# Expert rows packed block by block: fixed addresses for token loads and result stores in a routed transformer

## The chip, the cores and the metric

The kernel runs on one core of one Trainium2 chip. The metric is the device time of one execution in microseconds (us). The kernel before took 2116.01, 2119.6 and 2120.47 us in three runs, median 2119.6. Float32 is the type of inputs and outputs, a part of the attention works in bfloat16.

## The reference

The input is a batch of 4 sequences of 1024 tokens with 128 features. Two layers follow each other, each with a modulated layer norm before both halves. Layer 0 has attention with 16 heads over a window of 64 tokens, and then a mixture of 8 experts; layer 1 has full attention, then a block of its own with attention over the batch, and a mixture of 8 experts again. The part at hand is the mixture:

```python
logits = xf @ Wg.T + bg
probs = softmax(logits)
tp, ti = top_k(probs, 2)
h = gelu(einsum('td,efd->tef', xf, W1) + b1)      # DF = 512 in layer 0, 256 in layer 1
y = einsum('tef,edf->ted', h, W2) + b2
out = einsum('ted,te->td', y, w)                  # w: the two chosen probabilities
```

Every token needs only its two experts, so a kernel may send each token to those two and leave the other six out.

## The kernel before, in words

The engines are PE (matrix multiply), DVE (vector), ACT (scalar), POOL (GpSimd) and SP (which only issues transfers). The program is a row of stages with a barrier between them: start, `window_attention_stage` (78 to 619 us of the profile), the expert stages moe0b (620 to 746) and moe0c (752 to 881), `gather_qkv_stage`, full attention, cross attention, `last_norm_stage` (1797 to 1871), moe1b (1872 to 1962), moe1c (1967 to 2064) and the last gather (2068 to 2112).

**Parts and rows.** The batches are split in two parts of HB = 2 batches. A normalised token row is scattered twice, once per chosen expert, to the DRAM array `moe_rows` by an indirect DMA of POOL that takes a column of slots (`self.slot`) as row numbers: 16 scatters of 128 tokens per batch (`scatter`, `scatter_one`, lines 1531 to 1550). In `moe_rows` every expert of a part has a region of SPAN = 2048 rows of its own. So a batch's slot is known as soon as that batch is counted: `place` (line 1474) adds the expert's base, the count of the batches and tiles before, and the rank, and casts to integers. Its semaphore `placed` releases the batch's scatters. Unused rows must hold finite numbers, so `clear_rows` fills the array with zeros in the window attention, 19 DMAs of 960 KB on POOL's queue.

**Blocks.** `tabulate` (line 1505) runs once per part, after its second batch. It makes from the counts a table of NBK = 23 blocks of BR = 256 rows: which expert, and at which row the block begins. `block_stage` (line 1567) works through them: SP loads for each block the token rows (line 1604) and the expert's weights (line 1608, 578 KB in layer 0), PE turns the tokens (L1621), multiplies (L1632, L1642), ACT applies gelu (L1678), DVE copies (L1693, L1703, L1705), and ACT stores the result over the token rows (L1664), three blocks behind. Buffers for six blocks (XB, WBUF) let SP run ahead. Expert and row are read into registers by `load_four` (line 1560), four blocks at a time: one TENSOR_LOAD and eight register operations. SP calls it twice per four blocks, for experts and for rows, ACT once, for the rows of its stores.

**Work beside blocks.** Each expert stage takes an object whose methods run beside the blocks, called with the block's number j. In moe0b that is `RouteBeside` (line 1094): it routes the last batch (the norm, logits, probabilities, `compare`, `order`, `weights`, `place`, `tabulate`, spread over j = 0 to 13), and POOL scatters the last two batches, 11 scatters ahead of the second norm's `deviation`, 5 behind it, and 16 when the last batch is placed. In moe0c and moe1c it is `GatherBeside` (32 gathers of the first part's results), in moe1b `ScatterBeside` (line 1203, 32 scatters of the second part). POOL's method starts with the stage.

**The other scatters.** In the window attention DVE's and POOL's loops run over g, the groups of heads; `routed_at(g)` gives batch b - 1 a window of 32 steps. Batch 0's 16 scatters are issued in the window of b = 1, batch 1's in that of b = 2 (the last, 482 to 619 us), one per step between two multiplications of `probs` (L1061). In last_norm POOL scatters batches 0 and 1 as soon as each is placed, while DVE goes on with batches 2 and 3.

**Order.** Every engine executes its own list in the order of the code; nothing is reordered by a planner. Within `RouteBeside` the number j says beside which block a routing step stands.

## Time and profile before

| what | us |
|---|---|
| median of three runs (2116.01, 2119.6, 2120.47) | 2119.6 |
| the profiled execution | 2118.16 |
| its span | 2116.3 |
| PE busy | 1646.2 (78%) |
| DVE busy | 1357.7 (64%) |
| ACT busy | 1157.6 (55%) |
| POOL busy | 547.7 (26%) |

The sum of the prediction is made against the profiled execution, whose span can be read in the trace. Busy shares are averages over stages with different limits; the granted clock of PE was 0.874 of full speed in the mean. POOL's busy time has the issue of its indirect DMAs in it, SP's issues are not counted as busy. The software queue, which carries POOL's DMAs, moved 36.52 MB in 12464 packets, 5.0% of the 16 DMA engines' span.

### The profile page before, as it was taken

What the parts mean: (1) busy time and instruction counts of PE and PEld (TensorE: products, weight loads), DVE (VectorE), ACT (ScalarE), POOL (GpSimd) and SP (SyncE); (2) the same over time, 40 slices, a digit from 0 to 9 for tenths busy, and PEclk for the clock granted to TensorE, in tenths of its full rate; (3) what the DMA queues carried; (4) which work ended last, traced back from release to release, by engine and by line L of the source; (5) the groups of instructions that cost most, each with busy time, mean ns of one, the idle gap of its engine ahead of it and who ended that gap; (6) DMA issues with size and microseconds to landing.
All of it is one profiled execution on the core that took longest, in us unless ns stands there. A gap on an engine that the chain in (4) does not pass through costs nothing. (4 is left out here: it accounts for less than half of the span.)

```text
span 2116.3 us, 35460 instructions
## 1 busy us (share of the span) xinstructions
PE 1646.2 (78%) x11792; PEld 972.3 (46%) x11792; DVE 1357.7 (64%) x3360; ACT 1157.6 (55%) x3025; POOL 547.7 (26%) x620
## 2 busy tenths in 40 slices
PE   7799999999978849736999999999999543527280
PEld 3487778777768738611222222222222333416270
DVE  5654656666553305457999999999996468714062
ACT  3466766666644314331888888888888440202030
POOL 2133423525323244341001001001000100561505
PEclk8899999999989969865999999999999865558695
DMA  5144211111126446331000000000000000026362
GB/s 166 54 161 154 104 30 36 43 29 49 32 81 201 142 150 205 94 111 63 21 26 17 26 22 21 25 18 25 25 10 2 1 4 0 29 84 188 105 192 62
DMA packets 91569, 148.64 MB, mean 70 GB/s; under 512 B 18772, under 2 KB 59476, under 8 KB 91388
## 3 DMA queue, kind: packets, MB, share of 16 engines
q1 hardware_dynamic: 65676, 97.78, 15.8%
q0 software_dynamic: 12464, 36.52, 5.0%
q10 hardware_dynamic: 13248, 12.06, 1.7%
q8 instruction: 96, 1.57, 0.3%
q14 instruction: 85, 0.70, 0.1%
HBM read 82.25 MB, written 47.93 MB: 62 GB/s over the span
## 5 line engine op out<-in xcount | busy, mean ns | idle before, releaser
L2276 DVE TENSOR_REDUCE q_max<-s_ps 128x1 f32<-128x1024 f32 x512 | 598.1, 1219 | 14.0 <-PE s_ps L2167 6.6
L2257 ACT ACTIVATE probs<-s_ps 128x512 f32<-128x512 f32 x1024 | 535.5, 603 | 124.6 <-PE s_ps L2188 124.5
L2167 PE MATMUL s_ps<-k_stack,q_stack 64*128 64x512 bf16 x1024 | 351.4, 397 | 16.5 <-PEq L98 8.1
L2188 PE MATMUL s_ps<-q_stack,k_stack 64*128 64x512 bf16 x1024 | 319.7, 384 | 20.0 <-ACT probs L2257 15.6
L2202 PE MATMUL o_ps<-probs,v_aug 128*32 128x512 f32 x2048 | 273.6, 606 | 0.7 <-ACT probs L2257 0.7
L2188 PEld LDWEIGHTS s_ps<-q_stack,k_stack 64*128 64x128 bf16 x1024 | 78.4, 94 | 334.0 <-ACT probs L2257 282.1
L939 ACT ACTIVATE probs<-s_biased,s_min 128x128 f32<-128x128 f32 (+1 forms) x512 | 197.7, 391 | 39.7 <-DVE s_min L1032 38.3
L1061 POOL TENSOR_TENSOR probs<-probs,p_rsum 128x512 f32<-128x512 f32 x128 | 132.9, 1038 | 326.7 <-DVE p_rsum L1038 325.6
L804 PE MATMUL score_ps<-k_pad,q_bd 128*128 128x128 f32 x1024 | 145.9, 286 | 0.0
L1032 DVE CUSTOM_DVE_ANT_0 s_biased<-score_ps,nbias 128x128 f32<-128x128 f32 (+1 forms) x512 | 115.8, 282 | 40.4 <-PE score_ps L804 37.9
L1792 POOL CAST neg_max_parts<-neg_max 16x128 bf16<-16x128 f32 x32 | 9.0, 281 | 474.9 <-DVE neg_max L2284 474.9
L2167 PEld LDWEIGHTS s_ps<-k_stack,q_stack 64*128 64x128 bf16 x1024 | 77.3, 94 | 113.0 <-DVE q_max L2276 104.4
L804 PEld LDWEIGHTS score_ps<-k_pad,q_bd 128*128 128x128 f32 x1024 | 125.2, 192 | 7.4 <-issue 1.0
L962 DVE TENSOR_SCALAR q_bd<-proj_ps,qscale 64x512 f32<-64x512 f32 x64 | 48.5, 757 | 107.0 <-PE proj_ps L784 103.9
L1044 DVE COPY probsT<-probsT_ps 128x512 f32<-128x512 f32 x128 | 86.6, 677 | 35.9 <-PE probsT_ps L815 35.2
L939 ACT ACTIVATION_READ_ACCUMULATOR probs<-s_biased,s_min 128x1 f32 x512 | 98.0, 191 | 0.0
L889 ACT ACTIVATE q_bd<-proj_ps,qscale 64x512 f32<-64x512 f32 x64 | 43.7, 683 | 84.4 <-PE proj_ps L784 84.4
L1678 ACT ACTIVATE moe0c_hid<-moe0c_hps,moe0c_wblock 128x256 f32<-128x256 f32 x92 | 39.9, 473 | 86.5 <-PE moe0c_hps L1632 42.1
L815 PE MATMUL probsT_ps<-ident,probs 128*128 128x128 f32 x512 | 77.9, 275 | 4.6 <-POOL probs L1061 4.6
L830 PE MATMUL o_ps<-probsT,v_shift 128*64 128x64 f32 x1024 | 73.4, 234 | 9.2 <-ACT oT L947 8.6
L815 PEld LDWEIGHTS probsT_ps<-ident,probs 128*128 128x128 f32 x512 | 62.1, 142 | 37.8 <-issue 31.6
L1548 POOL DMA_INDIRECT moe_rows<-hk,moe_slot x64 | 66.7, 1042 | 43.4 <-DVE moe_slot L1494 28.8
(355 smaller groups left out, 2957.4 us busy)
## 6 DMA issues: line engine op xcount, KB each, us to landing
moe_rows<-zero_rows POOLq DMA_DIRECT2D x19, 960.0 KB
moe0b_wblock<-in_L_ffn_blocks SPq DMA_DIRECT2D x23, 578.0 KB
moe0c_wblock<-in_L_ffn_blocks SPq DMA_DIRECT2D x23, 578.0 KB
v_shift<-v_tiles SPq DMA_DIRECT2D x32, 256.0 KB
v_shift<-v_tiles SPq DMA_DIRECT2D x32, 224.0 KB
qk_parts_dram<-qk_parts SPq DMA_DIRECT2D x16, 384.0 KB
q_stack<-qk_parts_dram SPq DMA_DIRECT2D x192, 32.0 KB
k_stack<-qk_parts_dram SPq DMA_DIRECT2D x192, 32.0 KB
```

Of the source, the lines that this page charges most:

```text
L804: m = nc.tensor.matmul(sp_[g % 2][:, i, :], qbd[:, h % 2, j, :], kk[:, h % 2, BLK * j:BLK * j + P], start=True, stop=True)
L815: m = nc.tensor.transpose(tp[:, i, :], pr[:, k % 3, i, :], K.ident[:])
L830: m = nc.tensor.matmul(op[a * BLK:(a + 1) * BLK, i, :], src[:, a * HD0:(a + 1) * HD0], pt[:, k % 2, i, a * BLK:(a + 1) * BLK], start=True, ...
L939: r = nc.scalar.activation(pr[:, g % 3, i, own], sb_[:, g % 2, i, own], ACT.Exp, scale=-1.0, bias=mn[:, g % 4, i:i + 1], accum_out=sm[:, g ...
L1032: q = v.tensor_tensor_reduce(sb_[:, g % 2, i, own], sp_[g % 2][:, i, own], nbias[:, h % PAIRS, own], 1.0, 3e38, ALU.add, ALU.min, mn[:, g ...
L1044: v.tensor_copy(pt[:, k % 2], tp[:]).then_inc(pt_out, 1)
L1061: nc.gpsimd.tensor_tensor(pb, pb, bc(ri[:, g % 4, :], 2, P), ALU.mult).then_inc(normed, 1)
L2167: mm = nc.tensor.matmul(s1[u % 2][:, c * CH:(c + 1) * CH], qs[head_rows(m), quad % 4, j, qt * P:(qt + 1) * P], ks[head_rows(m), quad % 4, ...
L2188: nc.tensor.matmul(bank_of("exp", 4 * k + pos)[:], ks[head_rows(m), quad % 4, j, kt * P:(kt + 1) * P], qs[head_rows(m), quad % 4, j, half ...
L2202: m = nc.tensor.matmul(op[32 * h:32 * h + 32, :], va[:, quad % 2, kt, h, :], pr[:, k % 2, h, :], start=(kt == 0), stop=(kt == TPB - 1))
L2257: nc.scalar.activation(pr[:, k % 2, HEADS[pos], :], bank_of("exp", n)[:], ACT.Exp).then_inc(sm["exp"], 1)
L2276: v.tensor_reduce(mx[:, h % 4, col:col + 1], s1[u % 2][:], AX.X, ALU.max).then_inc(sm["maxed"], 1)
```

## The change

The rows of a part are packed block by block: expert after expert, each rounded up to whole blocks of 256 rows. Block j of part p then always begins at row (23 p + j) x 256, which is a constant of the program; only the expert, and with it the weights, is still picked by register.

- `moe_rows` has 2 x 23 x 256 = 11776 rows instead of 36480. The fill takes 23 DMAs of 256 KB.
- A slot is final only when both batches of a part are counted, since an expert's first block depends on the experts before it. `place` computes a rank within the expert (`rel`, in floats). `tabulate` computes the first row of each expert, and then per batch the slots (multiply with the choice, reduce, add), with a new semaphore `final` that the scatters wait for. The table keeps the experts alone.
- `load_four` is called once per four blocks by SP, and not at all by ACT. Token loads and stores have fixed addresses.
- In the window attention all 32 scatters of batches 0 and 1 move into the last window, at steps 2 to 31, with two behind the loop.
- `RouteBeside`: the routing steps stand closer: shift_logits at j = 7 (was 8), probabilities and compare at 8 (9), order and weights both at 9 (10 and 11), place and tabulate both at 11 (12 and 13). POOL computes both deviations first, and then issues all 32 scatters.
- In every expert stage POOL waits for the fourth token load (`x_in[3]`) before its work beside.
- In last_norm the code of POOL is unchanged, but its scatters now wait for `final`, so for `tabulate` of part 0.

The diff, without declarations of sizes and constants:

```diff
 NBKP = -(-NBK // 4) * 4
-PROWS = E * SPAN + (E - 1) * BR
-ROWS = 285 * P
-ZR = 5
+PROWS = NBK * BR
+ROWS = 2 * PROWS
+ZR = 4
 STEPS_OF = SPAN // BR
...
 
-        FILLS = ROWS // P // ZR // 3
+        FILLS = ROWS // P // ZR
 
         def clear_rows(pool, n):
 
             rows = K.moe_rows.rearrange("(p r) d -> p (r d)", p=P)
-            part = rows[:, 3 * n * ZR * D:3 * (n + 1) * ZR * D].rearrange("p (k z) -> p k z", k=3)
-            pool.dma_start(part, bc(zero[:], 1, 3)).then_inc(cleared, 16)
+            pool.dma_start(rows[:, n * ZR * D:(n + 1) * ZR * D], zero[:]).then_inc(cleared, 16)
 
...
                             N2.deviation(pool, b)
-                        if b >= 1 and at < 2 * TPB:
-                            if b == 1 and at == 0:
+                        if b == HB and at >= 2:
+                            if at == 2:
                                 pool.wait_ge(cleared, 16 * FILLS)
-                            M.scatter_one(pool, N2, b - 1, at)
+                            M.scatter_one(pool, N2, *divmod(at - 2, 2 * TPB))
+                for n in range(2 * TPB - 2, 2 * TPB):
+                    M.scatter_one(pool, N2, 1, n)
                 M.wait_scattered(pool, HB)
...
             N2.normalised_odd(dve, b)
+        elif j == 7:
+            M.shift_logits(dve, b, self.raw_logits)
         elif j == 8:
-            M.shift_logits(dve, b, self.raw_logits)
-        elif j == 9:
             M.probabilities(dve, b)
             M.compare(dve)
-        elif j == 10:
+        elif j == 9:
             M.order(dve)
+            M.weights(dve, b)
         elif j == 11:
-            M.weights(dve, b)
-        elif j == 12:
             M.place(dve, b, self.prior)
-        elif j == 13:
             M.tabulate(dve, 1)
...
             m.then_inc(M.logit_mm, 1)
-        elif j == 11:
+        elif j == 10:
             pe.wait_ge(M.chose, b + 1)
...
                              bias=M.affine[:, 1:2], scale=M.affine[:, 0:1]).then_inc(self.turn_out, 1)
-        elif j == 9:
+        elif j == 8:
             M.exponentials(act, b)
-        elif j == 12:
+        elif j == 11:
             act.wait_ge(M.prefixed, b + 1)
...
         N1.deviation(pool, b)
-        for n in range(11):
-            M.scatter_one(pool, N2, b - 1, n)
         N2.deviation(pool, b)
-        for n in range(11, 2 * TPB):
-            M.scatter_one(pool, N2, b - 1, n)
-        for n in range(2 * TPB):
-            M.scatter_one(pool, N2, b, n)
+        for k in (b - 1, b):
+            for n in range(2 * TPB):
+                M.scatter_one(pool, N2, k, n)
         M.wait_scattered(pool, B)
...
-        self.hot = K.sb(name + "_hot", [P, 2, TPB, E], ctx=st)
+        self.hot = K.sb(name + "_hot", [P, HB, 2, TPB, E], ctx=st)
-        self.place_f = K.sb(name + "_place", [P, 2, TPB], ctx=st)
+        self.rel = K.sb(name + "_rel", [P, HB, 2, TPB], ctx=st)
+        self.base_f = K.sb(name + "_base", [P, 2, TPB], ctx=st)
-         self.counted, self.placed, self.chain, self.scattered) = K.sems(
+         self.counted, self.placed, self.chain, self.scattered, self.final) = K.sems(
             st, name + "r", "router_in", "ones_set", "logit_mm", "shifted", "exp", "chosen", "prefix_mm", "counted", "placed",
+            "chain", "scattered", "final")
...
         dve.wait_ge(self.prefixed, b + 1)
-        ts = slice(b * TPB, (b + 1) * TPB)
-        part, first = divmod(b, HB)
-        base = self.cum[:, b - 1, :, TPB] if first else self.steps[:, part * E:(part + 1) * E]
-        step(dve, v.tensor_copy(self.tot[:, b % 2, :, 0], base))
+        if b % HB:
+            step(dve, v.tensor_copy(self.tot[:, b % 2, :, 0], self.cum[:, b - 1, :, TPB]))
+        else:
+            step(dve, v.memset(self.tot[:, b % 2, :, 0], 0.0))
         dve.wait_ge(self.counted, b + 1)
...
                                   ALU.add))
-        step(dve, v.tensor_tensor(self.picked[:], bc(self.slots[:], 1, 2), self.hot[:], ALU.mult))
-        step(dve, v.tensor_reduce(self.place_f[:], self.picked[:], AX.X, ALU.add))
-        v.tensor_copy(self.slot[:, :, ts], self.place_f[:]).then_inc(self.placed, 1)
+        step(dve, v.tensor_tensor(self.picked[:], bc(self.slots[:], 1, 2), self.hot[:, b % HB], ALU.mult))
+        v.tensor_reduce(self.rel[:, b % HB], self.picked[:], AX.X, ALU.add).then_inc(self.placed, 1)
 
...
         v, step = self.nc.vector, self.step
-        base, marks = self.steps[:, part * E:(part + 1) * E], self.steps[:, 2 * E:2 * E + STEPS_OF]
-        number = self.steps[:, 2 * E + STEPS_OF:]
+        marks, number = self.steps[:, 0:STEPS_OF], self.steps[:, STEPS_OF:]
         blocks, first, upto = (self.nb[:, i, :] for i in range(3))
-        passed, spent = self.le[:, 0], self.le[:, 1]
-        expert, row, rest = (self.tf[:, i, :] for i in range(3))
-        step(dve, v.tensor_tensor(first, self.cum[:, (part + 1) * HB - 1, :, TPB], base, ALU.subtract))
-        step(dve, v.tensor_tensor(self.over[:], bc(first, 2, STEPS_OF), bc(marks, 1, E), ALU.is_gt))
+        passed, expert = self.le[:], self.tf[:]
+        dve.wait_ge(self.placed, (part + 1) * HB)
+        total = self.cum[:, (part + 1) * HB - 1, :, TPB]
+        step(dve, v.tensor_tensor(self.over[:], bc(total, 2, STEPS_OF), bc(marks, 1, E), ALU.is_gt))
         step(dve, v.tensor_reduce(blocks, self.over[:], AX.X, ALU.add))
         g4 = self.pairs[:].rearrange("p (a b) -> p a b", a=E)
         step(dve, v.tensor_tensor(g4, bc(blocks, 1, E), self.low[:].rearrange("p (a b) -> p a b", a=E), ALU.mult))
         step(dve, v.tensor_reduce(first, g4, AX.X, ALU.add))
-        step(dve, v.tensor_tensor(upto, first, blocks, ALU.add))
+        v.tensor_tensor(upto, first, blocks, ALU.add)
+        step(dve, v.tensor_scalar(first, first, float(BR), float(part * PROWS), ALU.mult, ALU.add))
+        for i in range(HB):
+            b = part * HB + i
+            step(dve, v.tensor_tensor(self.picked[:].rearrange("p c t e -> p (c t) e"), bc(first, 1, 2 * TPB),
+                                      self.hot[:, i].rearrange("p c t e -> p (c t) e"), ALU.mult))
+            step(dve, v.tensor_reduce(self.base_f[:], self.picked[:], AX.X, ALU.add))
+            v.tensor_tensor(self.slot[:, :, b * TPB:(b + 1) * TPB], self.base_f[:], self.rel[:, i], ALU.add
+                            ).then_inc(self.final, 1)
+        dve.wait_ge(self.final, (part + 1) * HB)
         step(dve, v.tensor_tensor(passed, bc(upto, 1, NBK), bc(number, 2, E), ALU.is_le))
-        step(dve, v.tensor_tensor(spent, passed, bc(blocks, 1, NBK), ALU.mult))
-        v.tensor_reduce(expert, passed, AX.X, ALU.add)
-        step(dve, v.tensor_reduce(rest, spent, AX.X, ALU.add))
-        step(dve, v.tensor_tensor(rest, number, rest, ALU.subtract))
-        step(dve, v.tensor_scalar(rest, rest, float(BR), float(part * PROWS), ALU.mult, ALU.add))
-        step(dve, v.scalar_tensor_tensor(out=row, in0=expert, scalar=float(SPAN), in1=rest, op0=ALU.mult,
-                                         op1=ALU.add))
+        step(dve, v.tensor_reduce(expert, passed, AX.X, ALU.add))
         step(dve, v.tensor_scalar(expert, expert, float(E - 1), None, ALU.min))
-        step(dve, v.tensor_copy(self.table[:, part, :, 0:NBK], self.tf[:, 0:2, :]))
+        step(dve, v.tensor_copy(self.table[:, part, 0:NBK], expert))
 
     def scatter(self, pool, N, b, first, last):
 
-        pool.wait_ge(self.placed, b + 1)
+        pool.wait_ge(self.final, b + 1)
         N.wait_normalised(pool, (b + 1) * TPB)
...
         if n == 0:
-            pool.wait_ge(self.placed, b + 1)
+            pool.wait_ge(self.final, b + 1)
             N.wait_normalised(pool, (b + 1) * TPB)
...
             def _(pool):
+                pool.wait_ge(x_in[3], 16)
                 beside.gpsimd(pool)
 
             @block.sync
             def _(sp):
-                experts, rows = {}, {}
+                experts = {}
                 for j in range(NBK):
                     if j % 4 == 0:
-                        experts.update(load_four(nc, mybir.EngineType.SP, M.table[0:1, part, 0], j, E - 1))
-                        rows.update(load_four(nc, mybir.EngineType.SP, M.table[0:1, part, 1], j, ROWS - BR))
+                        experts.update(load_four(nc, mybir.EngineType.SP, M.table[0:1, part], j, E - 1))
                     if j >= XB:
                         sp.wait_ge(turned, j - XB + 1)
-                    sp.dma_start(xi[:, j % XB], K.moe_rows[bass.ds(rows.pop(j), BR), :].rearrange("(p a) d -> p a d", a=H)
+                    sp.dma_start(xi[:, j % XB], K.moe_rows[(part * NBK + j) * BR:(part * NBK + j + 1) * BR, :].rearrange("(p a) d -> p a d", a=H)
                                  ).then_inc(x_in[j % XB], 16)
...
             def _(act):
-                rows = {}
-
                 def store(k):
 
                     act.wait_ge(y_out, k + 1)
-                    act.dma_start(K.moe_rows[bass.ds(rows.pop(k), BR), :].rearrange("(p a) d -> p a d", a=H),
+                    act.dma_start(K.moe_rows[(part * NBK + k) * BR:(part * NBK + k + 1) * BR, :].rearrange("(p a) d -> p a d", a=H),
                                   ys[:, k % YB]).then_inc(stored[k % YB], 16)
 
                 for j in range(NBK):
-                    if j % 4 == 0:
-                        rows.update(load_four(nc, mybir.EngineType.Activation, M.table[0:1, part, 1], j, ROWS - BR))
                     if j >= 3:
```

How this moves instructions, first on POOL's queue in moe0b (`n0ba_rstd` and `n0bb_rstd` are the two deviations, the DMAs are scatters). Before:

```order
L147 TENSOR_TENSOR n0ba_rstd<-n0ba_ve,neghalf 128x8 [waits n0a_var_eps]
L1548 DMA moe_rows<-hk,moe0_slot 36480x128 [waits start_scales,start_cols_out,start_x_in3]
L1548 DMA moe_rows<-hk,moe0_slot 36480x128 x10
L147 TENSOR_TENSOR n0bb_rstd<-n0bb_ve,neghalf 128x8 [waits start_exp]
L1548 DMA moe_rows<-hk,moe0_slot 36480x128 x5
L1548 DMA moe_rows<-hk,moe0_slot 36480x128 [waits start_scales,start_cols_out,start_x_in3]
L1548 DMA moe_rows<-hk,moe0_slot 36480x128 x15
```

After:

```order
L147 TENSOR_TENSOR n0ba_rstd<-n0ba_ve,neghalf 128x8 [waits n0a_var_eps,win_probsT_out]
L147 TENSOR_TENSOR n0bb_rstd<-n0bb_ve,neghalf 128x8 [waits start_exp]
L1546 DMA moe_rows<-hk,moe0_slot 11776x128 [waits start_scales,start_cols_out,moe0r_final]
L1546 DMA moe_rows<-hk,moe0_slot 11776x128 x15
L1546 DMA moe_rows<-hk,moe0_slot 11776x128 [waits start_scales,start_cols_out,moe0r_final]
L1546 DMA moe_rows<-hk,moe0_slot 11776x128 x15
```

(Semaphores are shared between stages, so a wait can bear the name of an earlier stage's.) The groups of 11, 5 and 16 have become one row of 32, all behind `final`, and the second deviation no longer has scatters ahead of it.

Then SP's queue at the start of moe0b, where the ISA rows are register operations. Before:

```order
L1563 TENSOR_LOAD moe_table
L1563 ISA x8
L1563 TENSOR_LOAD moe_table
L1563 ISA x8
L1604 ISA
L1604 DMA moe0b_xin<-moe_rows 128x256
L1608 ISA
L1608 DMA moe0b_wblock<-in_L_ffn_blocks 128x1156
```

After:

```order
L1561 TENSOR_LOAD moe_table
L1561 ISA x8
L1602 DMA moe0b_xin<-moe_rows 128x256
L1606 ISA
L1606 DMA moe0b_wblock<-in_L_ffn_blocks 128x1156
```

One load of the table with its eight operations is gone ahead of the first token load, and one register operation at each token load. The same holds for every fourth block; over the program SP has 24 such loads instead of 48.

## Rows read from the trace of the kernel before

**Rows 1.** The page, first line: the span.
```profile
span 2116.3 us, 35460 instructions
```

**Rows 2.** Timeline of POOL in moe0b: start us, length us, instruction, idle before.
```profile
633.96 1.06 POOL L1548 DMA_INDIRECT moe_rows<-hk,moe_slot  x1 [0.20 <-issue]
...
646.70 0.95 POOL L1548 DMA_INDIRECT moe_rows<-hk,moe_slot  x1 [0.30 <-issue]
...
693.46 0.96 POOL L1548 DMA_INDIRECT moe_rows<-hk,moe_slot  x1 [28.78 <-DVE moe_slot L1494]
...
712.48 0.95 POOL L1548 DMA_INDIRECT moe_rows<-hk,moe_slot  x1 [0.30 <-issue]
```

**Rows 3.** Windows in moe0b: us, busy us (count) per engine, PEclk, DMA share, GB/s.
```profile
634.00:654.00 20.00, 12.73 (x76) 11.82 (x75) 5.30 (x12) 6.44 (x16) 10.60 (x11) 0.84 0.56 187
...
658.50:666.00 7.50, 7.50 (x56) 7.11 (x55) 2.30 (x9) 3.26 (x9) 4.87 (x5) 1.00 0.76 216
666.00:693.40 27.40, 27.40 (x195) 25.80 (x195) 13.51 (x41) 17.03 (x38) 0.00 (x0) 1.00 0.71 213
693.40:718.00 24.60, 14.06 (x78) 10.93 (x77) 6.51 (x22) 3.80 (x9) 15.41 (x16) 0.82 0.45 139
```

**Rows 4.** Windows of moe0c (first line) and of moe1b.
```profile
764.00:790.00 26.00, 10.77 (x51) 8.49 (x50) 1.00 (x3) 3.46 (x8) 13.21 (x14) 0.63 0.44 136
...
1877.00:1885.50 8.50, 7.29 (x28) 5.51 (x28) 1.63 (x3) 1.53 (x4) 6.37 (x8) 0.62 0.64 223
1885.50:1920.00 34.50, 6.28 (x24) 5.17 (x24) 1.84 (x4) 1.42 (x4) 20.73 (x22) 0.57 0.29 89
1920.00:1948.00 28.00, 28.00 (x196) 26.49 (x195) 12.35 (x28) 10.28 (x28) 0.00 (x0) 0.98 0.78 244
```

**Rows 5.** SP's table loads (L1563), 1872 to 1910: durations ns min/median/max, starts.
```profile
L1563 SPq FUSED_REGOPS  x16: 3/147/700, 1872.3 to 1890.9; - x16
...
L1563 SPq TENSOR_LOAD <-moe_table x4: 2/396/688, 1871.8 to 1885.9; - x4
```

**Rows 6.** Timelines at the start of moe1b (POOL, SP, PE) and of moe0b (SP).
```profile
1872.55 0.95 POOL L1537 DMA_INDIRECT moe_rows<-n1d_hat,moe_slot  x1 [8.20 <-POOLq L98]
...
1874.86 0.34 SPq L1604 DMA_DIRECT2D moe1b_xin<-moe_rows  x1
...
1876.99 0.69 PE L1621 MATMUL moe1b_xps<-ident,moe1b_xin 128*128 128x128 f32 x2 [25.64 <-DMA moe1b_xin<-moe_rows]
...
623.79 0.36 SPq L1604 DMA_DIRECT2D moe0b_xin<-moe_rows  x1
...
626.95 0.33 SPq L1604 DMA_DIRECT2D moe0b_xin<-moe_rows  x1
```

**Rows 7.** Timelines of POOL (first line) and DVE in last_norm.
```profile
1823.15 1.10 POOL L1537 DMA_INDIRECT moe_rows<-n1d_hat,moe_slot  x1 [12.98 <-DVE moe_slot L1494]
...
1831.70 0.17 DVE L1494 CAST moe_slot<-moe_place 128x16 uint32<-128x16 f32 x1
...
1835.49 0.19 DVE L1529 CAST moe_table<-moe_tf 128x46 int32<-128x46 f32 x1
...
1858.62 0.29 DVE L1493 TENSOR_REDUCE moe_place<-moe_picked 128x16 f32<-128x128 f32 x1 [1.11 <-DVE moe_picked L1492]
...
1870.68 0.19 DVE L1529 CAST moe_table<-moe_tf 128x46 int32<-128x46 f32 x1
```

**Rows 8.** Timelines of DVE (place) and of PE in moe0b.
```profile
691.52 0.17 DVE L1481 COPY moe_totals<-moe_cum 128x8 f32<-128x8 f32 x1
...
693.01 0.17 DVE L1494 CAST moe_slot<-moe_place 128x16 uint32<-128x16 f32 x1
...
699.97 0.41 PE L1621 MATMUL moe0b_xps<-ident,moe0b_xin 128*128 128x128 f32 x2 [1.36 <-issue]
```

**Rows 9.** Windows of batch 1 and batch 2 in the window attention.
```profile
212.67:346.55 133.88, 128.62 (x1247) 104.33 (x1245) 84.53 (x412) 91.78 (x352) 41.75 (x40) 1.00 0.19 60
346.55:481.85 135.30, 130.47 (x1246) 105.84 (x1245) 84.88 (x411) 91.90 (x352) 56.70 (x51) 0.99 0.15 38
```

More of the change, by code:

```diff
@@ L1306, in __init__ @@
         self.weight = K.sb(name + "_weight", [P, 2, NT], ctx=st)
-        self.table = K.sb(name + "_table", [P, 2, 2, NBKP], mybir.dt.int32, ctx=st)
+        self.table = K.sb(name + "_table", [P, 2, NBKP], mybir.dt.int32, ctx=st)
     def router_buffers(self, st):
@@ L1317, in router_buffers @@
         self.raw = K.sb(name + "_raw", [P, TPB, E], ctx=st)
-        self.steps = K.sb(name + "_steps", [P, 2 * E + STEPS_OF + NBK], ctx=st)
+        self.steps = K.sb(name + "_steps", [P, STEPS_OF + NBK], ctx=st)
         self.lg = K.sb(name + "_lg", [P, TPB, E], ctx=st)
@@ L1335, in router_buffers @@
         self.slots = K.sb(name + "_slots", [P, TPB, E], ctx=st)
-        self.place_f = K.sb(name + "_place", [P, 2, TPB], ctx=st)
+        self.rel = K.sb(name + "_rel", [P, HB, 2, TPB], ctx=st)
+        self.base_f = K.sb(name + "_base", [P, 2, TPB], ctx=st)
         (self.router_loaded, self.ones_set, self.logit_mm, self.shifted, self.exped, self.chose, self.prefixed,
-         self.counted, self.placed, self.chain, self.scattered) = K.sems(
+         self.counted, self.placed, self.chain, self.scattered, self.final) = K.sems(
             st, name + "r", "router_in", "ones_set", "logit_mm", "shifted", "exp", "chosen", "prefix_mm", "counted", "placed",
-            "chain", "scattered")
+            "chain", "scattered", "final")
         self.n = 0
@@ L1354, in table_buffers @@
         self.nb = K.sb(name + "_nb", [P, 3, E], ctx=st)
-        self.le = K.sb(name + "_le", [P, 2, NBK, E], ctx=st)
-        self.tf = K.sb(name + "_tf", [P, 3, NBK], ctx=st)
+        self.le = K.sb(name + "_le", [P, NBK, E], ctx=st)
+        self.tf = K.sb(name + "_tf", [P, NBK], ctx=st)
     def load_router(self, sp, A):
@@ L1453, in weights @@
         v, ts = self.nc.vector, slice(b * TPB, (b + 1) * TPB)
-        step, rank, hot = self.step, self.rank[:], self.hot[:]
+        step, rank, hot = self.step, self.rank[:], self.hot[:, b % HB]
         v.tensor_scalar(hot[:, 0], rank, 0.0, None, ALU.is_equal)
@@ L2646, in constants @@
     before = (np.arange(P)[:, None] < np.arange(P)[None, :]).astype(np.float32)
-    steps = np.concatenate([np.arange(E) * SPAN, PROWS + np.arange(E) * SPAN, np.arange(STEPS_OF) * BR,
-                            np.arange(NBK)]).astype(np.float32)
+    steps = np.concatenate([np.arange(STEPS_OF) * BR, np.arange(NBK)]).astype(np.float32)
     return {"identity": np.eye(P, dtype=np.float32), "neg_bias": neg.reshape(P, PAIRS, P),
```

## The prediction

> **What bounds the kernel now.** I read the page first, then cut the four expert stages (moe0b, moe0c, moe1b, moe1c) into stretches, then looked at single rows where a stretch was slow. The span is 2116.3 us [rows 1]. The sum is made against the profiled execution, 2118.16 us, which lies 1.4 us under the median of the three runs, 2119.6; that is inside their scatter of 4.5 us. A difference of 0.2% (4.2 us) is about what a measurement of this kernel can tell from none.
>
> The change touches only the expert rows, so the question is what sets the pace around them. In quiet stretches of moe0b PE is busy all the time: 27.40 of 27.40 us with 195 matmuls, 7.1 per us [rows 3]. In layer 1 the quiet pace is 196 in 28.00 us, 7.0 per us [rows 4]. In both stretches POOL issues nothing. Where POOL issues indirect DMAs back to back, one each 1.26 us [rows 2], the pace falls apart: 76 matmuls in 20.0 us, 78 in 24.6 us [rows 3], 51 in 26.0 us and 24 in 34.5 us [rows 4]. DMA engines are not full there: their share falls from 0.71 to 0.45 and from 0.78 to 0.29 [rows 3, 4]. What the rows show instead is that every step on the other engines becomes long: a register operation on SP takes up to 700 ns with a median of 147 [rows 5], and a DVE step of 0.29 us starts 1.11 us late, 1.40 us a step [rows 7]. I call this the slow stretch. The short stream of five scatters between 658.6 and 665 has none: 56 matmuls in 7.50 us, PE full [rows 3].
>
> So the time of an expert stage is its blocks at 7 matmuls per us, plus what the slow stretches take. **The change moves these streams and joins some; that decides, far more than the register instructions it saves.**
>
> **The loss per stream.** Eleven scatters, 633.96 to about 647.9, is a stream of 13.9 us [rows 2]. The window of 20.0 us around it holds 76 matmuls, worth 76/7.1 = 10.7 us: 9.3 lost. Sixteen scatters, 693.46 to 713.7, 20.2 us long [rows 2]: 24.6 - 78/7.1 = 13.6 lost. So a stream loses its length less 4.6 and less 6.6 us; I take less 5.6, the grace once per stream.
>
> **The change part by part**, against 2118.16.
>
> 1. *Window attention, +1.* All 32 scatters of batches 0 and 1 move to the last batch's window, still one per group of heads, so never back to back. A window with 16 of them took 135.30 us, one with none 133.88 [rows 9]: 1.4 for 16. The same 32 scatters stand in one window instead of two, so their sum is unchanged. The longer table computation of part 0 gains some 1.5 us of DVE work, of which at most all shows; two scatters come after the loop, at most 2.5 us. Bounds 0 and +4; +1 because the POOL queue now ends in the same kind of step. The fills, 23 of 256 KB for 19 of 960 KB, lie in the first two windows under this attention; their transfers hide there before and after: 0. If this cover were gone, four more issues of about 1.3 us would show, +5.
>
> 2. *moe0b, +13.6.* In front of the last batch's deviation stand 11 scatters, behind it 5, later 16. Now no scatter starts before both batches are counted, and all 32 go in one stream of 32 x 1.26 = 40.4 us. Loss 40.4 - 5.6 = 34.8, where now it is 9.3 + 13.6 = 22.9: **+11.9**. The price comes twice from grace given up: the 5 scatters that cost nothing join it. Bounds: 0 (rival B) and +17 (if the stream loses all of its length). The routing steps are also pulled together: *order* with *weights* beside one block, *place* with *tabulate* beside another. Tabulate takes 3.8 us (1831.87 to 1835.68) [rows 7] and behind it PE stood 1.36 us in moe0b [rows 8], so a block covers some 2.5 us of DVE work. Place takes 1.7 us [rows 8]. The new pair is 1.7 + 3.8 + about 0.8 for the slots' additions = 6.3, so 3.8 shows instead of 1.4; order with weights, each estimated at about a place's length, 3.5 together, shows 1.0 instead of 0: together **+3.2** (0 if two more blocks of slack take it up, +6 if both pairs meet half the slack). SP's start: its first four rows of the table need one load instead of two. From the first TENSOR_LOAD at 1871.8 [rows 5] to the first token load at 1874.86 [rows 6] both take 3.1 us, so **-1.5**. By the Trainium skill, "Runtime: NRT & Kernel Launch", Instruction fetch mechanics, such a load takes about 200 ns per register, 0.8 us for four, and the term would be nearer -2.0; the rows here have a median of 396 ns in a disturbed stretch for all four, so the rule is not borne out. Sum 11.9 + 3.2 - 1.5 = 13.6.
>
> 3. *moe0c, moe1b, moe1c, +1.5 each.* POOL now waits for the fourth token load before it starts its stream. In moe1b the first scatter is at 1872.55, before SP's first load at 1874.86 and PE's first matmul at 1876.99 [rows 6]. Loads of four blocks are issued in 3.2 us (623.79 to 626.95) [rows 6] and land 2.1 us later or more, so with 1.5 saved the stream starts at 1873.4 + 3.2 + 2.1 to 4 = about 1879 to 1880.5, 7 us later. The slow stretch ends 7 us later too. Against that PE starts 1.5 us earlier and has four blocks loaded that it can do undisturbed, where now it does two (28 matmuls) before 1885.5 [rows 4]: two more blocks, 28 matmuls, 4.0 us at 7.0 per us. Net 7 - 1.5 - 4.0 = +1.5. ACT loses its 9 register rows per four blocks and SP half of its own; they run beside PE except in the slow stretch, where they may give up to 3 us per stage. Bounds per stage -4 (grace counted twice, all register time back) and +5 (no more blocks done). Sum **+4.5**.
>
> 4. *last_norm, +6.5.* The scatters of part 0 start at 1823.15, when batch 0 is counted [rows 7]. They must now wait for batch 1's place, which ends at 1831.87, and for five more small operations and three for its slots, eight at about 0.27 (3.8 us over tabulate's 15 is 0.25): about 1834. The queue behind is POOL's own: 32 x 1.26 = 40.4, so the last is issued at 1874.4 and landed at about 1877.4 (3 us, an estimate between the 2.1 of rows 6 and 4). Now the stage ends with DVE's table at 1870.87 [rows 7] and the next one's first POOL row is at 1872.55, 1.7 later. After: 1877.4 + 1.7 = 1879.1, **+6.5**. DVE was in the slow stretch at 1858.62 [rows 7]; it comes later now, so DVE is done earlier and no longer last. Bounds +4 and +11 (slow stretch that hits DVE sooner, and its chain ends behind POOL).
>
> 5. *Removed register work elsewhere, 0:* SP's loads run ahead of PE, six blocks of buffers deep; the quiet stretches show PE full. If this cover were gone, 24 loads at 1.5 us would be worth 36 us, and the quiet stretches say that it isn't.
>
> Sum: 1 + 13.6 + 4.5 + 6.5 = 25.6, so 2143.8 profiled, **2144 us**.
>
> **The rivals.**
>
> *A, faster: the slow stretch comes of the burst at a stage's start.* In the first microseconds of moe0c, moe1b and moe1c a stream, eight loads and cold buffers come together; now the stream starts after four blocks have landed. For it: moe0b's five scatters in mid-flow, 658.6 to 665, hurt nothing [rows 3], and in last_norm the stretch reached DVE late, between 1835 and 1858 [rows 7]. Against: the 11 and 16 of moe0b also come in mid-flow and do hurt [rows 3]. If a stream's grace grew from 5.6 to some 16 us in these three stages, each gives 10.5 back: 2144 - 31.5 = 2112.5. It decides from a grace of about 14 us on, where 25.6 is used up. Chance 0.2.
>
> *B, the join costs nothing.* If the loss goes by scatters in the stream (27 of them, 22.9 lost) or by a queue that is drained anyhow, moe0b's +11.9 vanishes: 2132. Against it is 56 matmuls at full rate beside five scatters. [...] Chance 0.13.
>
> *C, slower still.* With the loads of the blocks already in flow, the grace of the three later streams is nothing, as no row shows a stream of 32 that starts in flow: 5 us more in each, and last_norm's upper bound, 4.5 more: 2144 + 19.5 = 2163. For it: 24 matmuls in 34.5 us is a full stop, and buffered blocks may stop with it. Chance 0.1.
>
> *D, the change doesn't do what it says.* The order of instructions shows SP's second table load gone and one POOL stream; only if none of the moved streams ends a wait would the time stay, 2118. Chance 0.05.
>
> **Chances and range.** The forecast holds 0.52, with its own range 2130 to 2158 from half and one and a half times its unknown terms. Faster by over 0.2% comes from A (0.19) and a sliver of the rest: 0.2. Within 0.2%: D and the edges of A and B: 0.07. Slower: the rest, 0.73. The range 2108 to 2163 leaves out the better half of A and what lies above C, 2 in 10 at most.
>
> **What would show it.** Right: in moe0b one stream of 32 with a window of about 40 us that holds few matmuls, and no loss before it; PE standing about 4 us behind place with tabulate; the first token load 1.5 us earlier after a stage's start; POOL's first stream row in moe1b 7 us after the stage's start, and a slow stretch as long as now; last_norm's first scatter near 11 us later than now in the stage, and a wait for the scatters as its end. Wrong: SP's register operations at 147 ns and a full PE beside the streams of moe0c, moe1b or moe1c (A), or a loss in moe0b under 25 us (B).

## The result and the profile after

The changed kernel took 2147.78 to 2153.36 us in four runs, median 2148.9, against a median of 2117.8 of the kernel before in the same comparison. The ratio is 1.015, interval 1.0129 to 1.017: slower by 31 us (27 to 36). The forecast was 2144, its step sum +25.6. All ratios compare undisturbed executions; a single one of the ten of e3_norm, described below, took 3202.91 us and is not in them.

The profiled execution took 2153.36 us, 4.5 over the median of its kernel, so the stage times below are rather high. The first lines of its page:

```profile
span 2151.5 us, 34676 instructions
## 1 busy us (share of the span) xinstructions
PE 1652.1 (77%) x11792; PEld 977.0 (45%) x11792; DVE 1355.5 (63%) x3356; ACT 1159.4 (54%) x3025; POOL 544.5 (25%) x624
```

The span is 35.2 us longer than in [rows 1], with the same number of matmuls. PE is busy for 5.9 us more (1652.1 against 1646.2), so most of the rest, 29.3 us, is PE standing. Where, is read from the first token loads of the four expert stages. The columns are the instruction's durations (min/median/max, ns), then first and last start. First the changed kernel:

```profile
L1602 SPq DMA_DIRECT2D moe0b_xin<-moe_rows x23: 53/431/1102, 627.6 to 740.4; - x23
L1602 SPq DMA_DIRECT2D moe0c_xin<-moe_rows x23: 13/431/1230, 771.4 to 874.7; - x23
L1602 SPq DMA_DIRECT2D moe1b_xin<-moe_rows x23: 326/432/1400, 1903.2 to 1979.9; - x23
L1602 SPq DMA_DIRECT2D moe1c_xin<-moe_rows x23: 6/431/547, 1999.2 to 2084.4; - x23
```

Then the kernel before, the two that the earlier rows don't have:

```profile
L1604 SPq DMA_DIRECT2D moe0c_xin<-moe_rows x23: 5/333/967, 753.8 to 853.6; - x23
...
L1604 SPq DMA_DIRECT2D moe1c_xin<-moe_rows x23: 2/333/702, 1969.0 to 2050.6; - x23
```

A stage starts 3.1 us ahead of its first token load before and 1.6 us ahead of it after (one load of four table words instead of two), so its start moved by the difference of the loads plus 1.5. With [rows 6] for moe0b and moe1b, and three marks between (the first gather behind moe0c, 884.02 before and 906.42 after; the first DVE row of last_norm, 1796.98 and 1818.98; the first gather behind moe1c, 2067.72 and 2103.14):

| stretch | forecast | measured |
|---|---|---|
| start to moe0b | +1 | 627.6 - 623.8 + 1.5 = +5.3 |
| moe0b | +13.6 | (771.4 - 753.8 + 1.5) - 5.3 = +13.8 |
| moe0c | +1.5 | +3.3 |
| the attention stages | 0 | -0.4 |
| last_norm | +6.5 | +7.8 |
| moe1b | +1.5 | (1999.2 - 1969.0 + 1.5) - (1903.2 - 1874.9 + 1.5) = +1.9 |
| moe1c | +1.5 | +3.7 |
| last gather | 0 | -0.2 |
| sum | +25.6 | +35.2 |

The joined stream in moe0b, POOL's timeline:

```profile
686.46 1.03 POOL L1546 DMA_INDIRECT moe_rows<-hk,moe_slot  x1 [33.36 <-DVE moe_slot L1521]
...
725.75 0.96 POOL L1546 DMA_INDIRECT moe_rows<-hk,moe_slot  x1 [0.30 <-issue]
```

and the windows around it and around the stream of moe1b:

```profile
651.00:678.00 27.00, 26.75 (x197) 25.37 (x195) 13.08 (x42) 15.73 (x34) 1.64 (x1) 1.00 0.70 219
678.00:690.00 12.00, 8.84 (x57) 8.11 (x58) 7.66 (x28) 3.52 (x9) 2.93 (x3) 0.96 0.52 158
690.00:732.00 42.00, 12.99 (x65) 10.01 (x64) 1.76 (x4) 4.16 (x9) 27.88 (x30) 0.62 0.28 90
732.00:764.00 32.00, 31.39 (x208) 29.47 (x206) 11.45 (x23) 13.32 (x32) 0.00 (x0) 0.92 0.37 122
...
1903.00:1915.00 12.00, 8.48 (x41) 7.17 (x42) 2.51 (x5) 2.29 (x6) 3.34 (x4) 0.67 0.73 230
...
1921.00:1955.00 34.00, 6.46 (x22) 5.05 (x22) 1.92 (x4) 0.77 (x2) 22.92 (x24) 0.55 0.25 75
```

Before the stream moe0b runs at full pace (197 matmuls in 27 us, 7.3 per us); in the 42 us from 690 there are 65, worth 9.2 us at the 7.1 per us of [rows 3]: 32.8 lost, where the forecast had 34.8. In moe1b the slow stretch is as long and as slow as in [rows 4], 22 matmuls in 34 us, only later.

The granted clock of PE is low in such a stretch too, 0.57 in [rows 4] against 0.98 in the quiet stretch behind it. That is not what costs: the 24 matmuls there kept PE busy for 6.28 us, where at the quiet pace of 7.0 per us they need 3.4. The clock accounts for at most 2.9 of the 31.1 us lost; the rest is PE standing.

In last_norm the end has gone over from DVE to POOL (timelines of POOL and DVE):

```profile
1856.01 1.10 POOL L1535 DMA_INDIRECT moe_rows<-n1d_hat,moe_slot  x1 [23.84 <-DVE moe_slot L1521]
...
1895.88 0.96 POOL L1535 DMA_INDIRECT moe_rows<-n1d_hat,moe_slot  x1 [0.30 <-issue]
...
1876.70 0.18 DVE L1527 CAST moe_table<-moe_tf 128x23 int32<-128x23 f32 x1
```

DVE is done at 1876.88, with no step at 1.40 us; the last scatter is issued 19 us later. So DVE worked for 20.9 us beside an unbroken stream without being slowed. In the kernel before, the stream of this stage had run since 1823.15 [rows 7] when the first slow step came:

```profile
1849.65 0.19 DVE L1456 TENSOR_SCALAR moe_hot<-moe_rank 128x64 f32<-128x64 f32 x1
1850.92 0.29 DVE L1457 TENSOR_TENSOR moe_picked<-moe_pb,moe_hot 128x128 f32<-128x128 f32 x1 [1.08 <-DVE moe_hot L1456]
```

That is 27 us into the stream. Here, where no blocks run, the grace is several times the 5.6 us that the prediction took from the streams beside moe0b's blocks. The stage began 22.0 us later than before, so the first scatter is 1856.01 - 1823.15 - 22.0 = 10.9 us later within it.

### The profile page after: what moved, and what is told of

The parts are those of the page before. It is cut to its first block and busy times, and to the rows that moved or that the text cites. A ratio compares the mean times of both kernels' runs of the same rounds, so it can differ in the third digit from the quotient of the medians.

```text
span 2151.5 us, 34676 instructions
## 1 busy us (share of the span) xinstructions
PE 1652.1 (77%) x11792; PEld 977.0 (45%) x11792; DVE 1355.5 (63%) x3356; ACT 1159.4 (54%) x3025; POOL 544.5 (25%) x624
## 5 line engine op out<-in xcount | busy, mean ns | idle before, releaser
L1672 ACT ACTIVATE moe0b_hid<-moe0b_hps,moe0b_wblock 128x256 f32<-128x256 f32 x92 | 39.5, 473 | 81.6 <-PE moe0b_hps L1630 45.3
```

The costliest lines, as they stand in the source:

```text
L1672: nc.scalar.activation(hid[:, j % 2, f, :], hp[n % 4][:, 0:BR], gelu, bias=bias).then_inc(g_out, 1)
```

## The experiments

Twelve kernels ran, each against the kernel before on its own chip. First the change is taken apart, then its supposed cause is. The edits are shown in part. The length of one stage scatters by some 2 us either way between profiles: moe0b takes 130.0, 128.9 and 133.5 us in three kernels that share it (before, e2_wait4, e3_norm), from its first token load to moe0c's.

### The joined stream alone (e1_join)

```diff
         N1.deviation(pool, b)
-        for n in range(11):
-            M.scatter_one(pool, N2, b - 1, n)
         N2.deviation(pool, b)
-        for n in range(11, 2 * TPB):
+        pool.wait_ge(M.placed, b + 1)
+        for n in range(2 * TPB):
             M.scatter_one(pool, N2, b - 1, n)
```

> The kernel before, with one edit: in moe0b POOL computes both deviations first and waits until the last batch is placed, then issues its 32 scatters in one stream (11, 5 and 16 before). My theory (a stream loses its length less a grace of some 5.6 us): about 12 us slower than before, 2117.8 + 12 = 2130, with one slow stretch of some 38 us in moe0b. Rival (the loss goes by the number of scatters in slow streams, or the join is hidden): within 3 us of before.

Ratio 1.0058 (1.0041 to 1.0075): +12 us, as expected. Its windows in moe0b:

```profile
634.00:654.00 20.00, 20.00 (x137) 18.78 (x136) 11.34 (x39) 11.88 (x29) 2.99 (x2) 0.96 0.79 248
...
690.00:735.00 45.00, 14.11 (x57) 10.15 (x57) 3.21 (x10) 3.47 (x8) 26.89 (x28) 0.58 0.28 91
```

The stretch that held 76 matmuls [rows 3] now holds 137; the long stream takes it back and more: it loses 45 - 57/7.1 = 37 us. This part of the change alone (the joined and later stream) makes the kernel slower, without any register, layout or routing step touched. Rival B falls.

### POOL's wait for the fourth token load, alone (e2_wait4) and taken out (e5_no_wait)

```diff
             def _(pool):
+                pool.wait_ge(x_in[3], 16)
                 beside.gpsimd(pool)
```

> The kernel before, with one edit: in all four expert stages POOL waits for the fourth token load before its work beside. My theory: in moe0c, moe1b and moe1c the stream and its slow stretch move 7 to 8.5 us later, two more blocks (4 us) are done before it; +3 to +4.5 us per stage, some +8 to +13 in all (moe0b: 0). Rival A (the slow stretch comes of the burst at the stage's start): faster than before by up to 30 us. Rival (the place of the stream doesn't matter): 0.

Ratio 1.0074 (1.0057 to 1.0091): +16 us, over the top of what I expected, and the other way than rival A. Its windows in moe1b:

```profile
1881.00:1893.00 12.00, 8.87 (x42) 7.15 (x42) 2.51 (x5) 2.28 (x6) 4.50 (x5) 0.72 0.66 218
1893.00:1930.00 37.00, 6.75 (x26) 5.94 (x27) 1.94 (x4) 0.77 (x2) 26.14 (x28) 0.57 0.29 93
```

Ahead of the slow stretch there are 42 matmuls where there were 28 [rows 4]: one block more, not the two I had counted. The slow stretch stays whole. In the profiles moe0c, moe1b and moe1c each take longer, by 5.0, 6.7 and 5.4 us. The reverse, in the changed kernel, with the changed kernel once more beside it (e6_after):

> The changed kernel without POOL's wait for the fourth token load. The wait alone cost the kernel before 16.6 us. My theory: the same here, 12 to 17 us under the changed kernel, since the streams start with the stage again. Rival (with four table words to load instead of eight, the wait is what lets blocks start early here): within 4 us of the changed kernel.

> The changed kernel once more, unedited, as the reference of this chip for the run without the wait: 1.013 to 1.017 of before.

Without the wait 1.0092 (1.0072 to 1.0111), with it 1.0144 (1.0125 to 1.0164), on one chip: the wait costs the changed kernel 0.0052 x 2122 = 11 us, with an uncertainty of some 6 from the two intervals. That is a little under the 12 to 17 expected, and over the rival's 4, which it doesn't exclude by itself; in the profiles the three stages are 4.8, 3.7 and 4.5 us shorter than in e6_after, which speaks for the higher price.

### last_norm alone (e3_norm)

```diff
+                pool.wait_ge(M.placed, HB)
                 for b in range(HB):
                     M.scatter(pool, N, b, 0, TPB)
```

> The kernel before, with one edit: in last_norm the scatters wait until batch 1 is placed, too (1831.9 instead of 1823.15; the change itself waits some 2.5 us longer, for the final slots). My theory: POOL's stream of 40.4 us ends the stage, and the time grows by 8.7 less the slack of now: last scatter issued at 1872.3, landed at 1875.3, next stage 1877; +4 to +5 us. Rival (DVE's chain still ends the stage, only less slowed): 0 or faster by up to 5.

Ratio 1.0016 (1.0006 to 1.0026): +3.4 us (1.3 to 5.5), somewhat under the range of 4 to 5; in the profile the stage itself grew by 5.4. POOL and DVE:

```profile
1836.62 1.10 POOL L1538 DMA_INDIRECT moe_rows<-n1d_hat,moe_slot  x1 [22.00 <-DVE moe_slot L1495]
...
1875.99 0.96 POOL L1538 DMA_INDIRECT moe_rows<-n1d_hat,moe_slot  x1 [0.30 <-issue]
1882.48 0.96 POOL L1538 DMA_INDIRECT moe_rows<-n1d_hat,moe_slot  x1 [5.54 <-issue]
...
1865.68 0.19 DVE L1530 CAST moe_table<-moe_tf 128x46 int32<-128x46 f32 x1 [1.21 <-DVE moe_tf L1529]
```

DVE's table is ready at 1865.87, POOL issues its last scatter of this stage at 1875.99 and the next stage's first at 1882.48: POOL ends the stage.

### The register work put back (e4_regs)

```diff
                         experts.update(load_four(nc, mybir.EngineType.SP, M.table[0:1, part], j, E - 1))
+                        dict(load_four(nc, mybir.EngineType.SP, M.table[0:1, part], j, E - 1))
...
                 for j in range(NBK):
+                    if j % 4 == 0:
+                        dict(load_four(nc, mybir.EngineType.Activation, M.table[0:1, part], j, E - 1))
```

> The changed kernel, with the register work put back: SP loads four table words twice per four blocks and ACT once, all of expert numbers, and the second ones are not used (the register operation per token load stays away). My theory: each stage starts 1.5 us later, 4 x 1.5 = +6 over the changed kernel, 2149 + 6 = 2155, and nothing more, since SP runs ahead. Rival (register work in the slow stretches holds the blocks back): +12 or more over the changed kernel.

Ratio to before 1.0193 (1.0174 to 1.0212), where the changed kernel has 1.0144 and 1.015: 9 to 10 us over it, with an uncertainty of some 6 from the two intervals. That leaves room for the 6 us of four starts and for some 6 more in the slow stretches, so the run doesn't decide between the two; it excludes that the register work is worth nothing, and that it is worth the 31 us that would have paid for the change.

### Is it the streams? Pauses between the DMAs

Every part but the last moved a stream. If the slow stretch is what costs, breaking the streams up must give back far more than the change took. First paced by the blocks (`blocks` counts the blocks whose tokens PE has turned), in moe0b alone (p2_pace0b), then in all four expert stages (p1_pace_all). The excerpt is the last batch's half of moe0b; the other half waits for block 3 + n // 2 in the same way, and the second deviation comes behind the first four scatters:

```diff
         for n in range(2 * TPB):
+            if n % 2 == 0:
+                pool.wait_ge(self.blocks, 14 + n // 2)
             M.scatter_one(pool, N2, b, n)
```

> The kernel before, with one edit: in moe0b POOL's 32 scatters are paced, two per block (it waits for the block's tokens to be turned by PE), the last batch's from block 14 on, and the second deviation comes after the first four. My theory (the slow stretch comes when indirect DMAs stand back to back for over some 5 us): the 22.9 us that two streams lose in moe0b mostly vanish, about 2120 - 20 = 2100. Rival (each scatter costs the blocks some 0.7 us wherever it stands: 22.9 over 32): 2120, as before.

> As p2_pace0b, and the 32 gathers of moe0c and moe1c and the 32 scatters of moe1b are paced the same way, two per block; the products, sums and norm steps beside the blocks stand later by up to six blocks. My theory: moe0c gives back about 20 us of its 22 lost; in layer 1 a block lasts 1.97 us and two DMAs 2.52, so sixteen blocks are held to 2.6 us (10 us) instead of the 33 lost now: 23 back in each; 2120 - 20 - 20 - 46 = about 2034. Rival (in layer 1 the DMAs stand nearly back to back, so the slow stretch comes all the same): 2080. Rival (cost per DMA): 2120.

0.9901 (0.9884 to 0.9919) and 0.9633 (0.9615 to 0.9651): 21 and 78 us faster than before, where 20 and 86 were expected. In p1_pace_all the steps that use the gathered rows (products, sums, parts of the norm) had to move up to six blocks later as well, so moe0c and moe1c hold two edits; moe0b and moe1b hold the pacing alone. One window of moe1b in the second, and the POOL rows in it:

```profile
1850.00:1885.00 35.00, 24.74 (x156) 21.66 (x156) 10.17 (x23) 8.53 (x24) 21.61 (x23) 0.95 0.70 208
```

```profile
1850.89 0.96 POOL L1555 DMA_INDIRECT moe_rows<-n1d_hat,moe_slot  x1 [1.55 <-DMA moe_affine<-in_L_ffn_ln_bias]
1852.16 0.96 POOL L1555 DMA_INDIRECT moe_rows<-n1d_hat,moe_slot  x1 [0.30 <-issue]
1853.42 0.96 POOL L1555 DMA_INDIRECT moe_rows<-n1d_hat,moe_slot  x1 [0.30 <-issue]
1854.68 0.96 POOL L1555 DMA_INDIRECT moe_rows<-n1d_hat,moe_slot  x1 [0.30 <-issue]
1857.02 0.96 POOL L1555 DMA_INDIRECT moe_rows<-n1d_hat,moe_slot  x1 [1.37 <-DMA moe_affine<-in_L_ffn_ln_bias]
```

About as many scatters as in [rows 4] (23 in 35 us against 22 in 34.5), but mostly in fours with gaps of 1.3 to 1.6 us between, and 156 matmuls instead of 24. So it isn't the number of DMAs. Their rate is somewhat lower: one per 1.52 us over the window, where the unbroken stream issues one per 1.26 until it ends at 1912.7, inside the window of [rows 4]. That rate alone doesn't decide either is shown by the drained kernels below.

Then drained wherever the blocks are (POOL waits until what it has issued has landed, gathers of moe0c and moe1c included), after every fourth (q1_drain4), after every eighth (q3_drain8), and after every fourth in the changed kernel (q2_after_drain4):

```diff
+    def scatter_drained(self, pool, N, b, n):
+        self.scatter_one(pool, N, b, n)
+        if n % 4 == 4 - 1:
+            pool.wait_ge(self.scattered, 16 * (2 * TPB * b + n + 1))
```

> The kernel before, with one edit: in the four expert stages POOL waits after every fourth scatter or gather until all it has issued have landed, wherever the blocks are. Theory D (the slow stretch comes when more DMAs of POOL are outstanding than four or five, so a drain prevents it): a group takes 5 us and a wait of some 2.5, so a stream of 32 lasts about 62 us and no stretch is slow; moe0b -18, moe1b -22, moe0c and moe1c some -8 each, as their products now wait for gathers: about 2120 - 56 = 2064. Rival (it was the slower rate beside the blocks or the tie to them that helped in the paced kernels, about one DMA each 1.3 to 1.9 us there): 2090 or more.

> As q1_drain4, with a drain after every eighth. Grace theory: a group of eight lasts 10.1 us and loses 10.1 - 5.6 = 4.5, so a stream of 32 loses 18 where it lost some 33; moe0b -9, the others -12 each: about 2120 - 45 = 2075, with short slow stretches in every group. Rival (the stretch needs some 11 or more DMAs): as fast as q1_drain4 or faster, no SP instruction at 700 ns.

> The changed kernel with the same edit, a drain after every fourth scatter or gather in the expert stages. If the joined stream of 32 is what the change costs in moe0b, its 35 us of loss go: -30; moe1b -24, moe0c and moe1c -8 to -10 each: 2152 - 72 = about 2080, within 15 us of q1_drain4 where the unedited pair stands 31 apart. Rival (the change costs for another reason than the streams): it stays 30 us over q1_drain4.

Every fourth 0.9742 (0.9721 to 0.9763), every eighth 0.9805 (0.9783 to 0.9826), the changed kernel with every fourth 0.9874 (0.985 to 0.9897). Windows of moe1b, first drained by four, then by eight:

```profile
1860.00:1900.00 40.00, 33.24 (x218) 29.84 (x217) 13.42 (x30) 11.09 (x32) 19.62 (x21) 0.95 0.72 235
```

```profile
1861.00:1900.00 39.00, 22.46 (x108) 19.30 (x108) 6.66 (x15) 5.70 (x16) 21.11 (x22) 0.74 0.53 170
```

218 matmuls in 40 us and 108 in 39, with 21 and 22 scatters: at nearly the same rate, the length of a run of DMAs decides how much PE gets done beside them. The kernel drained by eight issues its scatters at a lower rate than the paced one (one per 1.77 us against 1.52), and PE still does less beside them (108 matmuls in 39 us against 156 in 35). Both times came out within 4 us of what was expected (2064 and 2075; 2060 and 2073).

The third was not. I had expected the two drained kernels within 15 us of each other; they stand 0.0132 x 2116 = 28 us apart, about as the unedited pair. Windows of the changed, drained kernel in moe0b and in moe1b say why:

```profile
684.00:728.00 44.00, 40.98 (x274) 38.16 (x274) 15.95 (x35) 17.28 (x40) 23.73 (x24) 0.96 0.51 165
728.00:745.00 17.00, 0.01 (x1) 0.00 (x0) 0.42 (x1) 0.00 (x0) 7.66 (x8) 0.58 0.13 43
1881.00:1925.00 44.00, 40.88 (x277) 36.81 (x277) 21.96 (x47) 13.75 (x39) 23.35 (x25) 1.00 0.80 253
```

The blocks run beside the scatters at 6.2 to 6.3 matmuls per us, so the slow stretch is gone; but in moe0b POOL's scatters start so late (684, both batches counted) that they outlast the blocks, and PE stands from 728 to 745. A wait for POOL takes the place of a part of the slow stretch: moe0b is 7.8 us longer than in q1_drain4. The rest of the 28 us lies elsewhere. By the same marks as in the table above, moe0c is 5.8 us longer, moe1c 7.0, last_norm 9.3 (its scatters are drained in neither kernel), and moe1b 2.8 shorter. In moe0c, moe1c and last_norm POOL starts late as well, behind the fourth token load or the final slots. That the late start is what costs there fits, but no run takes the wait out of the drained kernel, so it isn't shown.

Last, the two kinds of pause together, paced by blocks but drained in moe1b (r1_best):

> p1_pace_all with one edit: moe1b's 32 scatters are drained after every fourth as in q1_drain4 instead of being tied to the blocks. The stage took 73.6 us paced and 69.7 us drained; the others were shorter paced. The two theories of the pauses agree here: about 4 us under p1_pace_all, 0.9615 of before, 2036 to 2044. Rival (stages are not independent: a longer stream at the end of moe1b delays moe1c by as much): 0.963, no gain.

0.964 (0.9608 to 0.9672), median 2038.5: not to be told from the paced kernel's 0.9633. In the profiles moe1b did shrink by the 4 us expected, from 77.0 to 73.0; the whole doesn't show it. Both beat the kernel before by 77 us and the changed one by over 100. What would come of pacing the scatters in last_norm wasn't tried.

## Why the prediction was right, point by point

**What bounds the kernel.** That streams of POOL's DMAs, not register work, set the pace of the expert stages was shown: breaking them up gave 78 us, joining two cost 12. The Trainium skill, "DMA: Bandwidth & Descriptors", SWDGE vs HWDGE vs iDMA, says that DVE can lock GpSimd out of the SBUF state in which it writes the descriptors of POOL's DMAs, and that DMAs issued from SP or ACT are immune to that interference. The section speaks of this one interference, and no run here shows it. It says nothing for or against the slow stretch, in which the steps of SP, PE and DVE beside a long stream become slow.

**Window attention, +1.** +5.3 in the profile. In the nine kernels with the old layout (the one before, three parts, five with pauses) SP's first table load lies at 620.6 to 622.7, in the five with the new one at 623.8 to 626.0, so some 3 us are real: the term was too small, inside its bounds of 0 to +4. Which of its pieces did it wasn't separated.

**moe0b, +13.6.** +13.8. The stream lost 32.8 us for 34.8; e1_join shows its +12 alone. The routing steps cost less than the 3.2 (the prediction's own terms, 3.8 instead of 1.4 and 1.0 instead of 0, add up to 3.4):

```profile
678.26 0.41 PE L1619 MATMUL moe0b_xps<-ident,moe0b_xin 128*128 128x128 f32 x2 [0.51 <-DVE moe0b_xT L1687]
...
688.82 0.44 PE L1619 MATMUL moe0b_xps<-ident,moe0b_xin 128*128 128x128 f32 x2 [2.90 <-DVE moe0b_xT L1687]
```

PE stood 0.5 us behind order with weights and 2.9 behind place with tabulate, 3.4 in all against 1.36 [rows 8]: +2.0. That the whole came out within 0.2 us is in part luck: 32.8 - 22.9 for the stream, 2.0 and -1.5 make +10.4, and the other 3.4 us lie outside the windows compared. From 732 us on 32.0 - 208/7.1 = 2.7 us are lost, where the stretch behind the stream lost 1.1 before:

```profile
718.00:745.30 27.30, 26.69 (x186) 25.13 (x184) 10.42 (x20) 11.82 (x28) 0.00 (x0) 0.97 0.35 117
```

The rest is within the 2 us by which a stage's length scatters.

**moe0c, moe1b, moe1c, +1.5 each.** +3.3, +1.9 and +3.7. The step that was mis-sized is "four blocks loaded that it can do undisturbed": the wait alone cost some 16 us in the kernel before, over 5 in each of three stages where my +7 - 4.0 gave 3. One block more was done before the slow stretch, not two, worth 2.0 us instead of 4.0. The stream also starts later than the 7 us that were assumed: in moe1b 1910.75 - 1901.6 = 9.2 us behind the stage's first table load, for 0.8 before, so 8.4 later. That makes 8.4 - 1.5 - 2.0 = +4.9. Measured was less, 1.9 to 3.7; the register work that is gone in the slow stretches may be the difference, which e4_regs leaves open.

**last_norm, +6.5.** +7.8 in the profile, and the mechanism as described: first scatter 10.9 us later in the stage, POOL last, DVE out of the slow stretch. The part of it that e3_norm has, 8.7 us of waiting out of 11, gave +3.4.

**The parts against the whole.** 12 + 16 + 3.4 for the three waits, less 9 to 10 for the register work, plus 2 and 3 for routing steps and window attention, are 27 us; measured were 31 (27 to 36 by the interval). The parts close within their uncertainty, which is some 8 us. With the wait at 11 us, as it was measured in the changed kernel, they are 22: what a part costs depends on the others.

**The rivals.** A fell with e2_wait4, whose sign was the other one; B with e1_join; D with the timelines. C asked for no grace where the blocks are already in flow, and some 5 us more per stage. Two windows of moe1b in the changed kernel, from the stream's first scatter at 1910.75 on, answer it:

```profile
1910.70:1916.00 5.30, 5.12 (x35) 4.51 (x34) 1.75 (x4) 1.90 (x5) 4.03 (x5) 0.97 0.78 266
1916.00:1921.00 5.00, 1.79 (x13) 1.34 (x11) 0.00 (x0) 0.38 (x1) 3.78 (x5) 1.00 0.60 179
```

For 5.3 us PE goes on at 6.6 matmuls per us, then it falls to 2.6: the grace is there. The sum came out at +31 instead of +45.

What stays open is the cause of the slow stretch itself. The runs show what it hangs on (the length of a run of POOL DMAs without a pause), not which resource fills up. Nor is the length of the run all of it: beside the blocks of moe0b and moe1b a stream slows the others after some 5 us, in last_norm, where no blocks run, after 27. What the blocks add (their loads, their stores, their semaphores) was not varied.

## What to carry to other kernels

Look at the matmuls per us beside POOL's indirect DMAs, not at DMA bytes: where they stand back to back beside other work for over some 5 us, the other engines' instructions themselves may be slow, and a pause after every four (a wait until they have landed, or until a block has gone by) can be worth more than a layout (here 2.6 and 3.7% gained against 1.5% lost). A layout that saves register loads, but needs all counts before the first scatter, pays for it with later and longer streams: price the start and the end of the stream, and who waits for it, before the instructions saved.

## What was not expected of the hardware

A gap of 1.3 to 1.6 us after mostly four scatters was enough to keep PE at 156 matmuls in 35 us, where an unbroken stream left 24 in 34.5.

A fixed address made the issue of SP's loads no cheaper. Its token load has a median of 431 ns with the address as a constant and 333 ns with it in a register (the rows of the stages above); with the MOVE of 29 ns and the register operation of 37 ns that went away, the issue of one load is 32 ns dearer. ACT's stores went the other way, from 338 ns and a MOVE of 29 to 326. The rows of the loads before, and of the stores of moe0c before and after:

```profile
L1604 SPq FUSED_REGOPS  x92: 3/37/711, 623.6 to 2050.5; - x92
L1604 SPq MOVE moe0b_xin<-moe_rows x23: 12/29/700, 623.7 to 721.6; - x23
...
L1664 ACTq MOVE moe_rows<-moe0c_y x23: 29/29/38, 786.0 to 880.0; - x23
L1664 ACTq DMA_DIRECT2D moe_rows<-moe0c_y x23: 338/338/377, 786.1 to 880.0; - x23
...
L1660 ACTq DMA_DIRECT2D moe_rows<-moe0c_y x23: 326/326/331, 786.5 to 900.8; - x23
```
